# In a graph network's update stage, counts summed by ScalarE, and the features and one loop message folded into a TensorE product

## The reference

```python
in_deg = segment_sum(ones(e), dst, num_segments=n)
loop_message = where((in_deg > 0)[:, None], h @ loop_weight, h @ evolve_loop_weight)
W = (W3 @ a)[:, 0]
rel_e = rel_emb[etype]                                   # 200 relations
score = h[src] @ w_src + h[dst] @ w_dst + rel_e @ w_rel
alpha = exp(leaky_relu(score))[:, None]
alpha = alpha / sum(alpha, axis=1, keepdims=True)
msg = (h[src] + rel_e) @ weight_neighbor * alpha
agg = segment_sum(msg, dst, num_segments=n)
return relu(agg) + loop_message                          # added to x, h = layernorm(x)
```

## Time and profile before

| What | Value |
|---|---|
| Time, median of 3 runs | 2484.68 us (2482.67 to 2486.18) |
| The profiled execution: its own time, its span | 2481.11 us, 2479.4 us |
| Busy: PE, DVE, ACT, POOL | 1745.3, 1847.3, 646.7, 1414.4 us |
| Update stage, 2200 to 2256 us: DVE, PE, ACT busy | 51.11, 38.01, 17.19 of 56 us |
| Edge stage, 1700 to 1900 us: PE, DVE, ACT, POOL busy | 132.41, 152.06, 118.10, 152.76 of 200 us |
| Mean granted TensorE clock | 0.812 of 2.4 GHz |

### The profile page before, as it was taken

How to read it: one execution, slowest core, us unless ns; L and a number is a source line. 1 busy time by engine, 2 the same in 40 slices (tenths; PEclk the granted TensorE clock), 3 DMA queues, 4 the chain that set the end, 5 groups by cost and what they waited for, 6 DMA issues and landing times. The chain is left out here.

```text
span 2479.4 us, 40425 instructions
## 1 busy us (share of the span) xinstructions
PE 1745.3 (70%) x9773; PEld 1304.6 (53%) x9773; DVE 1847.3 (75%) x4758; ACT 646.7 (26%) x1852; POOL 1414.4 (57%) x1202
## 2 busy tenths in 40 slices
PE   0699667777777735589998865466666666667997
PEld 0599534444444424488888853233333333345776
DVE  8988598888898876586666636677777777776395
ACT  0000200000000001111111114465555565524331
POOL 0388377777777720248888820477777777710200
PEclk9999866767667655799999977688778887668999
DMA  3011345445444421678989971477777777731101
GB/s 101 1 4 3 88 122 131 131 131 131 122 119 126 128 38 53 225 259 267 281 262 272 279 227 66 146 204 204 205 201 205 202 203 202 184 42 37 27 0 52
DMA packets 213517, 352.16 MB, mean 142 GB/s; under 512 B 49280, under 2 KB 123452, under 8 KB 213308
## 3 DMA queue, kind: packets, MB, share of 16 engines
q0 software_dynamic: 74368, 167.86, 26.9%
q1 hardware_dynamic: 138140, 180.51, 23.7%
q10 hardware_dynamic: 928, 2.75, 0.3%
HBM read 324.66 MB, written 26.36 MB: 142 GB/s over the span
## 5 line engine op out<-in xcount | busy, mean ns | idle before, releaser
L1016 POOL DMA_INDIRECT e_rows<-table,e_gidx x904 | 899.1, 995 | 277.0 <-issue 250.7
L1256 PE MATMUL e_psO<-e_rows,e_oh 128*128 128x260 f32 x880 | 362.8, 573 | 36.6 <-DVE acc L1081 32.2
L1081 DVE TENSOR_TENSOR acc<-acc,e_psO 128x260 f32 (+1 forms) x672 | 331.7, 494 | 35.8 <-PE e_psO L1256 5.2
L1256 PEld LDWEIGHTS e_psO<-e_rows,e_oh 128*128 128x128 f32 x880 | 222.2, 276 | 121.2 <-DVE acc L1081 69.7
L1157 PE MATMUL e_psA<-e_own_of_unit,e_ohT 128*128 (+2 forms) x904 | 107.6, 178 | 249.0 <-DVE e_ohT L1054 134.2
L2025 PE MATMUL e_psO<-e_rows,e_oh 128*128 128x456 bf16 x464 | 213.2, 459 | 90.2 <-DVE e_oh L1987 90.2
L1157 PEld LDWEIGHTS e_psA<-e_own_of_unit,e_ohT 128*128 128x128 bf16 x904 | 80.3, 99 | 361.6 <-issue 352.7
L675 POOL DMA_INDIRECT records<-ordered,s_chunk x68 | 153.2, 2253 | 112.1 <-ACT ordered L656 92.0
L1927 ACT ACTIVATE away<-iota_b,etype 128x200 bf16<-128x200 bf16 x464 | 176.0, 449 | 3.4 <-issue 0.3
L649 PE MATMUL sort_ps<-work 125*109 125x64 f32 x850 | 159.8, 390 | 21.4 <-DVE work L639 15.4
L1580 POOL DMA_INDIRECT ln_xn<-token_rows,slot_row x64 | 99.8, 1560 | 125.9 <-POOLq L102 104.5
(11 more groups left out here) (381 smaller groups left out, 3613.8 us busy)
## 6 DMA issues: line engine op xcount, KB each, us to landing
hot_run<-in_L_ffn_w_dram SPq DMA_DIRECT2D x107, 512.0 KB
XN<-in_L_ffn_w_dram SPq DMA_DIRECT2D x85, 512.0 KB
e_edge_row<-edge_rows SPq DMA_DIRECT2D x116, 256.0 KB, 4.1
e_rows<-table,e_gidx POOLq DMA_INDIRECT x904
e_edge_row<-edge_rows SPq DMA_DIRECT2D x110, 128.0 KB
table<-frow SPq DMA_DIRECT2D x25, 192.5 KB
table<-frow SPq DMA_DIRECT2D x25, 130.0 KB, 1.9
token_rows<-ln_xn SPq DMA_DIRECT2D x25, 128.0 KB, 1.7
```

The source lines that it names most:

```text
L1016: pool.indirect_dma_start(out=rows[:, r, t, 0:width], out_offset=None, in_=table, in_offset=bass.IndirectOffsetOnAxis(ap=gidx[:, r, t:t + ...
L1081: v.tensor_tensor(d, d, psO[:, units * (r % (4 // units)) + j, 0:accw], ALU.add).then_inc(S["added"], 1)
L1256: return pe.matmul(out[:, 0:A0], oh[:, r, t, :], rows[:, r, t, :], start=start, stop=stop)
```

## The change

In the dense stage VectorE subtracts the evolve weights from the loop weights, so that `wl` holds their difference and the evolve weights. In the edge stage TensorE adds, by a product with the identity, the tile of X to the evolve half of `psL`, so `loops` then holds the excess of one message over the other, and the evolve message plus X. In the update stage the reduction and the two mask operations go; `cnt` is copied with an accumulated output, its row sum, and ScalarE takes the sign of that; VectorE makes X in one operation, excess times sign plus the rest, where two stood before.

```diff
--- before.py
+++ after.py
@@ -1840,6 +1840,8 @@
                             if last is not None:
                                 rests(last)
                         dn.pipeline(dve, 2, 2, step)
+                        dve.wait_ge(wl_loaded, 32)
+                        link(v.tensor_tensor(wl[:, :, 0:D], wl[:, :, 0:D], wl[:, :, D:2 * D], ALU.subtract))
                         dve.wait_ge(dn.used, NT)
                         split_own(link, 1)
 
@@ -2012,8 +2014,10 @@
                     pe.wait_ge(staged_ready, q)
                     pe.wait_ge(loop_kept, q)
                     for j in range(KD):
-                        ins = pe.matmul(psL[:, :], staged[:, j, :], wl[:, j, :], start=(j == 0), stop=(j == KD - 1))
-                    ins.then_inc(looped, 1)
+                        pe.matmul(psL[:, :], staged[:, j, :], wl[:, j, :], start=(j == 0), stop=False)
+
+                    pe.matmul(psL[:, D:2 * D], ident[:, :], X[:, bass.ds(q - 1, 1), :].rearrange("p a d -> p (a d)"),
+                              start=False, stop=True).then_inc(looped, 1)
 
             def l1_sync(sp, S):
                 sp.wait_ge(S["acc_zero"], 2)
@@ -2041,7 +2045,7 @@
             psG = ps("psG", [P, 2, 512], c)
             chain, updated = sem("chain5"), sem("updated")
             cready, cturned, ccopied, gsum = sem("c_ready"), sem("c_turned"), sem("c_copied"), sem("g_sum")
-            added, clamped, looped = sem("u_added"), sem("u_clamped"), sem("u_looped")
+            added, looped, received = sem("u_added"), sem("u_looped"), sem("u_received")
             pipeline, locate, back = by_tiles
 
             with nc.Block() as block:
@@ -2050,30 +2054,26 @@
                     v = nc.vector
                     link = Chain(dve, chain).link
 
-                    link(v.tensor_reduce(deg[:, 0, :], acc1[:, :, D:A1], AX.X, ALU.add))
-                    link(v.tensor_scalar(deg[:, 0, :], deg[:, 0, :], 0.0, None, ALU.is_gt))
-                    link(v.tensor_scalar(deg[:, 1, :], deg[:, 0, :], -1.0, 1.0, ALU.mult, ALU.add))
-
                     def update(s, dyn):
                         t, q, r = locate(s, dyn, 0)
                         b = r % 2
                         at = bass.ds(t, 1)
-                        xt, agg, loop, evolve = (m.rearrange("p a w -> p (a w)") for m in (
+                        xt, agg, excess, evolved = (m.rearrange("p a w -> p (a w)") for m in (
                             X[:, at, :], acc1[:, at, 0:D], loops[:, at, 0:D], loops[:, at, D:2 * D]))
 
-                        v.scalar_tensor_tensor(xt, loop, deg[:, 0, at], xt, ALU.mult, ALU.add).then_inc(looped, 1)
+                        dve.wait_ge(received, t + 1)
+                        hold(dve, "dve")
+                        v.scalar_tensor_tensor(xt, excess, deg[:, 1, at], evolved, ALU.mult, ALU.add).then_inc(looped, 1)
                         dve.wait_ge(gsum, t + 1)
 
                         v.tensor_tensor(upd[:, r, :], psG[:, b, 0:D], agg, ALU.add).then_inc(added, 1)
-                        dve.wait_ge(looped, t * 2 + 1)
-                        v.scalar_tensor_tensor(xt, evolve, deg[:, 1, at], xt, ALU.mult, ALU.add).then_inc(looped, 1)
                         if not isinstance(t, int) or t >= 1:
 
                             dve.wait_ge(updated, t)
                             hold(dve, "dve")
                             halves(t - 1, 1)
                         dve.wait_ge(added, t + 1)
-                        dve.wait_ge(looped, t * 2 + 2)
+                        dve.wait_ge(looped, t + 1)
 
                         v.scalar_tensor_tensor(xt, upd[:, r, :], 0.0, xt, ALU.max, ALU.add).then_inc(updated, 1)
                     pipeline(dve, 0, 0, update)
@@ -2092,6 +2092,10 @@
                             nc.scalar.activation(cntT[:, r, 0, :], psC[:, r % 2, 0:P], ACT.Copy)
                             nc.scalar.activation(cntT[0:R - P, r, 1, :], psC[0:R - P, r % 2, P:2 * P], ACT.Copy)\
                                 .then_inc(ccopied, 1)
+                            act.wait_ge(cready, t + 1)
+                            hold(act, "act")
+                            nc.scalar.activation(deg[:, 1, bass.ds(t, 1)], deg[:, 0, bass.ds(t, 1)], ACT.Sign)\
+                                .then_inc(received, 1)
                         if soon is not None:
 
                             t, q, r = soon
@@ -2099,7 +2103,7 @@
                             hold(act, "act")
                             nc.scalar.activation(cnt[:, r, :],
                                                  acc1[:, bass.ds(t, 1), D:A1].rearrange("p a w -> p (a w)"),
-                                                 ACT.Copy).then_inc(cready, 1)
+                                                 ACT.Copy, accum_out=deg[:, 0, bass.ds(t, 1)]).then_inc(cready, 1)
                     pipeline(act, 2, 0, step)
 
                 @block.tensor
```

## The result

| | Kernel before | Changed kernel |
|---|---|---|
| Time, median (range, runs) | 2485.43 us (2482.67 to 2488.36, 4) | 2471.21 us (2467.66 to 2474.85, 4) |
| The profiled execution, its span | 2481.11, 2479.4 us | 2474.85, 2473.1 us |
| Dense stage | 106.9 us | 107.4 us |
| Edge stage | 625.5 us | 628.4 us |
| Update stage | 53.9 us | 42.5 us |

The ratio of the times is 0.9943, 95% interval 0.9924 to 0.9962: 14.2 us less, where I had forecast 3.5 less. The two profiled executions lie only 6.3 us apart; the update stage alone gives 11.4, and the rest of this one execution of after is 5 us longer: 3 in the other stages of the table and 2 ahead of the dense stage.

The account below looks back on a forecast made before the run. VectorE was taken to hold the update stage, next the ScalarE-TensorE turn at 1.47 us. Steps sum to -1.21 us, the stage ends 3.46 earlier, other stages cost 0: 2481.2 us, 8 in 10 within 2473.5 to 2488.

Parts of the forecast that it names:

- Rival A: Update stage: VectorE stays the bound, TensorE's gap of over 2 us may go; -14.2 us, 2470.5 us; chance 0.12.
- I take it for the sequencer's fetch of instructions: Update stage: TensorE's idle of over 2 us between transposes and product, once in five tiles, is instruction fetch, not VectorE.
- The gap steps: Update stage: four steps between tiles' transposes containing TensorE's idle of over 2 us, sum 15.22; three lose 0.63 each, -1.89.
- The slow-clock steps stay: Update stage: five steps between transposes at TensorE's low clock, 10.21 us in sum, keep their length.
- The bank had long been free: Update stage: the `psG` bank was free well before the delayed product, so TensorE's idle of over 2 us wasn't VectorE's.
- VectorE's part: Update stage: without L2069, 0.39 us per tile and 9.8 us in all, VectorE's tile falls from 1.78 to 1.39 us.
- d: ScalarE's additions to its turn with TensorE: sign 0.10 plus accumulated output 0.15, 0.25 us, bounds 0.05 and 0.40.
- Rival D: ScalarE's accumulated output costs much more than 0.2 us, say d = 0.6: 2486.4 us, about 2 us lost; chance 0.10.
- the seven steps that VectorE had held: Update stage: seven steps held by VectorE's bank, 11.76 us, become 7 x 1.47 = 10.29, -1.47.
- C: Edge stage: the identity product's 18 us of TensorE work is all exposed; +14.8 us, 2499.5 us; chance 0.06.
- B: Update stage: TensorE's clock stays down, steps of 1.47 us become 2.13; +7.7 us, 2492.4 us; chance 0.08.
- The low end of its range: Update stage: the forecast's sum with d = 0.05, giving -6.6 us.

Follow-up runs that it names:

- third bank: Kernel before with a third psG bank, taken by the last tile of each ring of five: 2721.01 us, ratio 0.9988.
- counts alone: Kernel before with ScalarE summing counts and taking the sign; VectorE keeps two operations on X, no identity product: 2721.74 us, ratio 0.9996.
- its extensions: Whole change without identity product (2473.77 us), with four (2473.59), with a third psG bank (2474.19), and with that bank plus the sign behind the next `cnt` (2473.89).
- The fold alone: Kernel before with X in the psL product and one VectorE operation on X; reduction and one mask stay on VectorE: ratio 0.9961, again 0.9949.
- the last experiment: Kernel before with X in the psL product, reduction and one mask kept on VectorE, and a third psG bank: 2475.02 us, ratio 0.9958.
- two experiments: Whole change without the identity product: 2473.77 us, ratio 0.9961; whole change with that product done four times: 2473.59 us, ratio 0.9956.

## Why the prediction was wrong

I forecast 2481.2 us and put 0.12 on what happened. Rival A, VectorE stays the bound and the gap goes, had 2470.5; the median is 2471.21. That the two are 0.7 us apart is in part chance: the update stage gave 11.4 of A's 14.2 us, and the interval of the ratio allows 9.4 to 18.9 us less.

**The step that failed** is "I take it for the sequencer's fetch of instructions", against a row that said `<-DVE upd L2067`, and with it "The gap steps: ..., so three of them lose 0.63 each" and "The slow-clock steps stay". The runs show the shared bank in its place: the product of a ring's first tile waits for VectorE's addition of the tile just before, and with a third bank these four waits are gone. Sorted as the prediction sorted them, the 24 steps between the first and last transposes (2205.68 to 2243.16 us, 37.48 us, 47.12 before):

| Steps | Before | Forecast | Measured |
|---|---|---|---|
| Four at a ring's start | 15.22 | 13.33 | 7.30 |
| The three slow ones behind two of these | 6.32 | 6.32 | 4.14 |
| The other seventeen | 25.58 | 26.11 | 26.04 |
| Sum | 47.12 | 45.76 | 37.48 |

The first line holds 6.0 of the 8.3 us that the sum was off, the second 2.2. The third agrees by chance: ScalarE's additions were shorter than forecast, and the low clock at the stage's start held longer. The steps lost 9.64 us; with 0.05 given back at the stage's start (0.15 forecast) and 1.78 more gained at its end (2.25 forecast) the stage is 11.4 us shorter, not 3.5. "The bank had long been free" came of taking two banks for two tiles of distance. With a ring of five it is one tile at r = 0. That VectorE's addition ended 0.14 or 0.15 us ahead of the product four times out of four could have been read from the trace of before.

The argument that I had against A, "the gap stands also where TensorE wasn't held (2231.39 to 2234.32)", was the same error: TensorE's transposes had not been held there, but its product was, by VectorE's addition that ended at 2233.24.

**That the slow steps went** is in A's 24 steps of 1.39 us too, and its cause stays open. The kernels that keep VectorE's 1.78 us (the one before, third bank, counts alone) have slow spells in the middle of the stage; of the whole change and its extensions there are seven profiles, and none has one: from 8 us into the stage the clock reads 1.00. The fold alone has one spell, in one of its two profiles. In the profiles of these kernels, 16 waits for the bank were over 1.3 us; 11 were followed by a stretch at 0.50, five were not, and one more stretch at 0.50 followed a wait of 1.1 us (third bank). What decides between these I can't tell from the rows. The Trainium skill (TensorE: Matmul & The Clock Gate, A second HAM failure mode: psum-queue depth-cycling) tells of a kernel whose engine idles briefly as it goes through PSUM banks and whose clock swings between half and full; the trace agrees with it by the clock of 0.57 right behind a wait of 1.45 us for a bank.

**VectorE's part was right.** 1.39 us per tile, as worked out from starts. Of the 14.2 us of rival A the stage gave 11.4; the missing 2.8 stand in the starts of its additions, of which these are the first two:

```profile
2209.76 0.42 DVE L2069 TENSOR_TENSOR upd<-psG,acc 128x256 f32<-128x256 f32 x1 [2.19 <-PE psG L2125]
...
2211.90 0.42 DVE L2069 TENSOR_TENSOR upd<-psG,acc 128x256 f32<-128x256 f32 x1 [0.85 <-PE psG L2125]
```

The first comes 4.60 us into the stage, 0.3 later than A had it. The step to the second takes 2.14 us in place of 1.39, since its product ran at the low clock. The four places where a ring begins take 2.3 us more than 1.39 per tile, and of these the third bank gave back about 1.6 us (42.5 to 40.9); the rest is near what VectorE's own loop cost in the last experiment. Its tail is 0.35 us shorter than A's 1.9.

**ScalarE's additions were a little too high.** d is 0.19, not 0.25: the sign 0.10 as costed, the accumulated output 0.09 where I took 0.15 (turn 1.22 before, 1.41 with both, 1.31 with the sign moved out). Rival D is out. For the seven steps that VectorE had held, about 1.41 stands in place of 1.68 on average. VectorE waited for a product in four tiles, not in most, as I had named for a sign: at 1.39 us it is all but level with the turn.

**The edge stage and the weights** cost nothing that shows, as forecast, and C is out by two experiments. The dense stage's lengths with and without the subtraction overlap. B did not occur: from 8 us into the stage the clock is 1.00.

**What each half is worth.** The fold gives 42.4 to 43.8 us of stage, the counts alone 52.8, both together 42.0 to 42.5, from 52.8 to 53.9. So the fold holds nearly all of it. The counts save VectorE 5.7 us, but those lay beside TensorE's slow start. That is what the prediction said of the start, and it missed the bank in what it said of the tiles.

**Three slips in the prediction's arithmetic** did not decide anything. The low end of its range, -6.6 us, has turns of 1.27 us, below VectorE's own 1.39, which would have held them; held at 1.39, the 15 steps make that end about -5.0. It called the gain at the stage's end nearly half of the whole, and by its own terms that is 2.25 of 3.46, two thirds. And its additions for the stage's end give 2250.12 where it wrote 2250.15, those of A 2239.3 where it wrote 2239.4.

## What to carry to other kernels

Where a ring of odd length shares two banks by parity, the first tile of a ring waits for the tile just before it, so any lateness of the engine that frees the bank comes through there in full: before one explains such a wait by something else, compare the releaser's end with the waiter's start at every one of those places. Where two engines seem to share the hold, find which one the other's waits end with: taking 0.39 us per tile, 9.8 us in all, from VectorE took 9.0 to 11.5 us off the stage. A long reduction at a stage's start is worth little while the next engine's first results come late anyway: 5.7 us of VectorE's work were worth at most 1.1 here.

## What the runs showed of the hardware

- ScalarE's accumulated output is an instruction of its own, ACTIVATION_READ_ACCUMULATOR, of 0.19 us, that starts 0.26 us after the copy of 200 columns and makes the turn 0.09 us longer.
- A sign of one column from SBUF lasts 0.20 us and adds 0.10 to ScalarE's queue.
- 57 us more of TensorE's work than the change has, in the stage of the gathers, left its length at 628.0 us (628.4 with the change).
- VectorE, with 1.39 us of work per tile, idled 0.25 to 0.29 us where its loop turns, for nothing that the profile shows.
- The same kernel took 2485 us on one chip and 2722 us on another. The changed kernel's profiled executions are 244 us apart, and its edge stage has 124 of them (752 for 628); in 400 us of that stage the third-bank kernel made 253 gathers there, the kernel before 310 elsewhere. Nearly all of the rest, 121 us, lies ahead of the dense stage, where the first layer gathers too; I did not look for its cause there.
- The granted clock fell to 1.2 GHz behind 11 of 16 waits of 1.3 to 2.2 us, and behind one of 1.1 us, at different places in two profiles of one kernel.
